# A decoder layer on one core: context tiles 2 and 3 loaded among the weights, small late loads behind context tile 5, and the order of steps written anew

## The reference

```
x = layernorm(x + self_attention(x))              # 16 heads of 16, rotary on q and k, softmax, output weights
x = layernorm(x + cross_attention(x, ctx, ctx))   # 16 heads of 64, causal mask and source length, softmax
x = layernorm(x + experts(x))                     # router to 14 experts, top 1, 256 -> 512 -> gelu -> 256
```

## Time and profile before

| | |
|---|---|
| median of the runs | 537.02 us |
| the profiled execution | 539.74 us |
| its span | 538.0 us |
| PE busy | 465.9 us (87%) |
| DVE, ACT, POOL busy | 340.5, 310.7, 210.8 us |
| PE idle, 0 to 91.39 us | 38.3 us |
| PE idle, 101 to 423.70 us | 4.0 us |
| mean granted clock of PE | 0.935 |

### The profile page before, as it was taken

The page is one execution under the profiler, slowest core; times in us unless marked ns, Lnnn a source line. Parts: engine busy times, 40 slices in busy tenths (PEclk is TensorE's granted clock), DMA queues, the critical chain, the costliest instruction groups (busy, mean ns, idle before and its releaser), DMA issues. The chain is left out here.

```text
span 538.0 us, 12482 instructions
## 1 busy us (share of the span) xinstructions
PE 465.9 (87%) x4364; PEld 399.7 (74%) x4364; DVE 340.5 (63%) x950; ACT 310.7 (58%) x1403; POOL 210.8 (39%) x294
## 2 busy tenths in 40 slices
...
GB/s 163 192 162 31 2 20 307 150 217 110 81 148 66 175 31 20 189 166 207 28 182 37 159 27 15 214 20 23 25 22 45 312 278 96 361 374 373 71 26 16
DMA packets 43033, 69.19 MB, mean 129 GB/s; under 512 B 12167, under 2 KB 33144, under 8 KB 42251
## 3 DMA queue, kind: packets, MB, share of 16 engines
...
## 5 line engine op out<-in xcount | busy, mean ns | idle before, releaser
L1025 ACT ACTIVATE probs<-bank,neg_max 100x100 f32<-100x100 f32 x512 | 169.8, 368 | 35.0 <-DVE neg_max L1151 26.3
L932 POOL TENSOR_TENSOR probs<-probs,row_inv 100x400 f32<-100x400 f32 x128 | 111.2, 888 | 129.1 <-DVE row_inv L1156 129.0
L1025 ACT ACTIVATION_READ_ACCUMULATOR probs<-bank,neg_max 100x1 f32 x512 | 118.1, 231 | 0.0
L1151 DVE TENSOR_REDUCE neg_max<-bank 100x4 f32<-100x400 f32 x128 | 67.7, 564 | 9.7 <-PE bank L1452 8.4
L1463 PE MATMUL bank<-ident,probs 100*100 100x100 f32 x512 | 68.3, 256 | 3.1 <-DVE probsT L1163 1.7
L1463 PEld LDWEIGHTS bank<-ident,probs 100*100 100x100 f32 x512 | 50.8, 130 | 15.8 <-issue 6.2
L1163 DVE COPY probsT<-bank 100x400 f32<-100x400 f32 x71 | 40.5, 571 | 22.7 <-PE bank L1463 21.8
L1378 PE MATMUL bank<-yT,W_Q 128*128 128x250 f32 (+1 forms) x224 | 50.7, 369 | 0.0
L1034 ACT COPY probsT<-bank 100x400 f32<-100x400 f32 x57 | 28.3, 496 | 37.1 <-PE bank L1463 33.6
L1304 PE MATMUL bank<-cT_h,W_K 128*128 128x250 f32 (+1 forms) x224 | 47.6, 297 | 1.5 <-DVE qk L1103 0.9
L1701 ACT ACTIVATE hT<-bank,b1c 128x128 f32<-128x128 f32 x72 | 20.5, 368 | 38.7 <-PE bank L1651 38.7
...
## 6 DMA issues: line engine op xcount, KB each, us to landing
expert_rows<-c_empty ACTq DMA_DIRECT2D x13, 1935.0 KB, 8.8
...
```

The source lines that it names most:

```text
L932: probs_ready.mark(pool.tensor_tensor(v, v, r, ALU.mult), step)
L1025: i = act.activation(probs[:, k % SLOTS, w], sc_bank[p % 2 * 2 + u][0:T, w], ACT.Exp, bias=neg_max[:, k % SLOTS, h:h + 1], accum_out=row_s ...
L1151: max_ready.mark(dve.tensor_reduce(neg_max[:, k % SLOTS, :], src, AX_X, ALU.max, negate=True), step)
```

## The change

Four things differ.

- The text of `block.sync`: Wout (piece 2) stands behind V (5, 6) instead of ahead of K. `load_c(2)` stands behind it, and `load_c(3)` between Q (7, 8) and WO (9, 10). `c_load.2` and `c_load.3` have left the list.
- The loads of `less`, `token_id`, `v_bias` and `Wr` are a function `load_late()`, called from the step `c_load.5`.
- The list `STEPS` is written anew from the first line to the last. It has 1686 steps instead of 1688, and the same work.
- With it some steps go to another engine: `w_lo.3` from POOL to DVE, `w_lo.6` from DVE to POOL, and many copies between ACT and DVE.

```
                 load_c(0)
                 load_x(2)
-                load_piece(2)
                 for k in (3, 4):
                     load_piece(k)
                 load_c(1)
...
                 for k in (5, 6):
                     load_piece(k)
+                load_piece(2)
+                load_c(2)
                 bc = lambda ap, n, w: ap.rearrange("(o n) -> o n", o=1).broadcast_to([n, w])
...
-                for k in (7, 8, 9, 10):
+                for k in (7, 8):
                     load_piece(k)
-                for dst, src in ((less[:, :], c_less), (token_id[:, :], c_token)):
-                    sp.dma_start(dst, src).then_inc(route_in, 16)
...
+                load_c(3)
+                for k in (9, 10):
+                    load_piece(k)
+                def load_late():
+                    for dst, src in ((less[:, :], c_less), (token_id[:, :], c_token)):
+                        sp.dma_start(dst, src).then_inc(route_in, 16)
...
                     elif kind == "c_load":
                         load_c(n)
+                        if n == 5:
+                            load_late()
```

```
-keys_v.4 turn.s.2.0.0 norm.s.2.0.1 K_out_v.0.3 pv.s.1.1 inv.s.2.1 V.0.1 norm.s.2.1.0 copy_a.s.2.0.0 o_hi.s.1.1 norm.s.2.1.1 o_lo.s.1.1 turn.s.2.0.1
+K.0.0 rot_sum.1 w_lo_p.5 scores.s.0.0 w_hi.6 K_out_v.0.0 qkT.1 max.s.0.0.0 w_lo_p.6 qk.2 max.s.0.0.1 qkT_out_a.1 max.s.0.1.0 w_hi.2 keys_v.1 K.0.1
```

337 lines of the change are left out of this document (168 added, 169 removed).

## The result

| | before | after |
|---|---|---|
| median of the runs | 537.75 us (20 runs, 536.57 to 540.14) | 534.79 us (20 runs, 531.76 to 537.54) |
| ratio | | 0.9943, 95% interval 0.9929 to 0.9957 |
| profiled execution | 539.74 us | 534.44 us |
| its span | 538.0 us | 532.7 us |
| mean granted clock | 0.935 | 0.938 |

The change makes the kernel faster, by 3.0 us in the medians and 5.3 us between the two profiled executions. The forecast was 518.1 us, and the range 510 to 527 doesn't hold the result.

What follows compares the result with a forecast made beforehand. PE bounds the kernel, after one early hole from a late context load. Gains 17.9 - 1.0 + 2.0 = 18.9 us take the profiled 539.74 to 520.8, or 518.1 us for the median; 8-in-10 range 510 to 527.

Steps and rivals of the forecast that it cites:

- The hole, and the loads: Near the start, PE's 18.7 us wait for context tile 2 goes whole; later WO loads cost nothing, with thin cover.
- Start to the scores of sequence 1: `scores.s.0.0` at 29.3 us, full clock back at 38.2, `scores.s.1.0` at 44.5 instead of 59.27, bounds 40 and 50.
- the 75.4: Forecast time in us of `scores.s.4.0`, 17.9 us ahead counting work moved across that point.
- The late loads: Eleven transfers put behind context tile 5 delay `v_bias` and input tile 4: cost 1.0 us, bounds 0 and 5.
- `scores.s.4.0` after 80 us: Sign, at the scores of sequence 4, that the forecast is wrong in size; 75.4 us was expected.
- ACT's wait before `vb_hi.0` over 2 us: Sign at ACT's wait for `v_bias`; the forecast wanted it under 2 us.
- the wait goes to the late loads: Rival: ACT waits at `vb_hi.0` and PE at xT.4, 4 us more than taken, 522 us; chance 0.13.
- more comes back: Rival: full clock early, no dip at 95 us, end shorter by 3.7 us, giving 510 us; chance 0.17.
- The long stretch: From 101 to 423.70 us, PE nearly always busy: change of 0, bounds -3 and +6 us.
- the fourth rival: New order loses in the long stretch through pauses at two PSUM banks; 1.8 us per tile makes 541 us; chance 0.05.
- The end: Last sequence before the experts: moved `wo.11` and `scores.x.15.0` gain 2.0 us, bounds -3.7 and +1.8.
- Sum: Whole kernel: 17.9 - 1.0 + 2.0 = 18.9 us gained, forecast 518.1 us.

Runs made afterwards that it cites:

- experiment 4: The changed list with the loads of before: Wout ahead of K, context tiles 2 and 3 behind WO and the late loads; 523.78 us, ratio 0.9739.
- experiment 1: The changed kernel with `load_late()` back behind WO, ahead of the first load of the list; 524.64 us, ratio 0.9758.
- experiment 2: The changed kernel with the transfers clearing the experts' rows asked for two sequences later, late loads left behind context tile 5; 529.61 us, ratio 0.9849.
- experiment 3: The kernel before with its own list and late loads, but context tiles 2 and 3 early and Wout behind V; 530.99 us, ratio 0.9871.
- experiment 5: The kernel before with its own list, Wout and late loads in place, only context tiles 2 and 3 asked for early; 522.00 us, ratio 0.9693.
- experiment 11: First 277 steps of the new list with `w_lo.9` and `rot.6` moved, then the order of before, on the loads of before; 520.31 us, ratio 0.9672.

## Why the prediction was wrong

**The hole, and the loads: right.** No wait for `cs` is left, as forecast, and WO isn't waited for (0.2 us on ACT). The second had luck in it: a context tile took SP 1.5 to 2.3 us and not the 3.67 of the sum, so that WO was asked for by 39.3 us and not 44.9. PE was 4.9 us ahead of the sum, and with the later loads the working has 2 to 3 us of waiting there. That the context must be loaded earlier for it was wrong for this list: experiment 4 has the same time with the loads of before.

**Start to the scores of sequence 1: right, and too careful.** `scores.s.0.0` came at 27.90 us (forecast 29.3), `scores.s.1.0` at 39.62 (44.5, bounds 40 to 50). The clock came back at 30 us and not at 38, 1.00 in the window 30 to 31:

```profile
28.00:29.00 1.00, 1.00 (x12) 0.93 (x16) 0.86 (x2) 0.00 (x0) 1.00 (x2) 0.50 0.55 149
29.00:30.00 1.00, 1.00 (x13) 0.50 (x5) 0.41 (x1) 0.00 (x0) 1.00 (x1) 0.64 0.97 253
30.00:31.00 1.00, 1.00 (x7) 0.81 (x5) 1.00 (x3) 0.73 (x2) 0.41 (x1) 1.00 1.15 224
```

I had taken the 11.6 us that the clock needed behind a hole of 18.7 us and laid them on a start at which PE hadn't stopped for long (its longest wait from 15 to 28 us was 1.4 us). It didn't stay at full clock: behind the waits for POOL at 49.15 and 50.94 us the clock was 0.52 from 50 to 55 us, and the mean from `scores.s.1.0` to `scores.s.3.0` is 0.85. `scores.s.4.0` in experiment 1, which has no late loads in the way, stands at 72.6 us, 2.8 earlier than the 75.4.

**The late loads: the step that failed.** "I take a cost of 1.0, bounds 0 and 5." It was 10: 534.79 against 524.64 us on different chips, 0.9943 against 0.9758 by the ratios. This term alone takes the result out of the range, since experiment 1 lies in it. Two of the signs that the prediction named came with it: `scores.s.4.0` after 80 us (82.3), and ACT's wait before `vb_hi.0` over 2 us (7.36). Of the three parts of the term two were too small.
- SP's time. I counted 6.7 us, from a stretch in which the clearing didn't run. It was 14.1. Of the 7.4 more, experiment 2 takes away 6.9 by moving the clearing. The place was named in the working ("starts at the same place"), and the direction too, but its price was left inside the bound of 5. The section of the Trainium skill named there (DMA: Bandwidth & Descriptors, Issuing engines are not separate DMA queues) was the one to follow. The trace agrees: with ACT's 1.9 MB beside them even SP's own rows of asking get longer, 3.66 instead of 0.34 us.
- PE's work. I set 13 us between cT.3 and xT.4; cT.3 ran at 59.99 us and PE was through at 72.40, 12.4. That part was right.
- What follows a hole. The sum had no term for the clock. Behind the 8.70 us PE was at 0.50 until 87 us, and what that costs can be read: 11.0 us at `scores.x.0.0` against experiment 1, of which the wait itself is 8.7.

The rival "the wait goes to the late loads" had the mechanism and the two waiters by name, ACT at `vb_hi.0` and PE at xT.4. It had a chance of 0.13 and a price of 4 us. A fair sum (14.5 us of queue even without contention, against 13 of work, in front of an engine that, before, worked at half the clock for 11.6 us behind a hole) should have made it likelier than "more comes back".

**The long stretch: 0 forecast, 4.7 lost**, within its bounds of -3 and +6. The cause isn't the one of the fourth rival (many pauses at the two banks): 2.4 of the 3.2 us of new idle time are one wait behind a move of V. That the list is the cause is shown by experiments 3, 5 and 11, in which the stretch is 269.7, 269.3 and 269.1 us with the old order in it. That this one wait is worth 2.4 us is not shown: moving `rot.6` gave 0.7 of it, and the rest stays behind the move. For the 1.5 us of busy time I have no cause.

**The end: a gain of 2.0 forecast, 0.6 lost** from `scores.x.12.0` to the experts. I added up two moved steps and let the clock out; its mean there is 0.67 after (418.80 to 448.80) and 0.72 before.

**Sum.** 18.9 forecast; start 2.8 more, late loads 10 less (they cost some 11 and not 1), long stretch 4.7 less, end 2.6 less: 4.4, and the profiled executions show 5.3. The reading of the profile was right on what bounds the kernel; it stopped at the first hole, and didn't ask of each load that was put off whether its queue had room at its new place.
